# Perceiver block, one core: VectorE's routing, small copies and rounding change places, and eight scatters run ahead of the scan inputs

## What is computed

```python
x = x + xattn(layernorm(x), ctx)   # int8-rounded q and output projection, 16 heads, 1601 keys
x = x + mamba(layernorm(x))        # x_proj, softplus(dt), scan over 128 steps as h = a*h + bx, y + x*D
x = x + moe(layernorm(x))          # 64 experts, top 8, capacity 512 rows each; silu(g)*u, down
def _qdq(x):
    s = jnp.maximum(jnp.max(jnp.abs(x), axis=-1, keepdims=True) / 127.0, 1e-08)
    return jnp.clip(jnp.round(x / s), -127.0, 127.0) * s
...
pos = jnp.arange(P) - starts[e_sorted]
valid = pos < C
xbuf = jnp.zeros((E, C, D)).at[e_sorted, pos].set(x[tok_sorted], mode='drop')
```

## Time and profile before

| what | us |
|---|---|
| median of 3 runs | 2214.68 |
| lowest and highest | 2214.42, 2221.53 |
| the profiled execution, its own time | 2217.85 |
| its span, first to last instruction | 2216.1 |
| start of the first strip's exponential | 37.3 |
| start of the last strip's exponential | 1710.7 |
| pair i = 8, exponential of its first strip to that of the next pair's | 106.3 |

### The profile page before, as it was taken

How to read it: one execution, slowest core, us unless ns; L and a number is a source line. 1 busy time by engine, 2 the same in 40 slices (tenths; PEclk the granted TensorE clock), 3 DMA queues, 4 the chain that set the end, 5 groups by cost and what they waited for, 6 DMA issues and landing times. The chain is left out here.

```text
span 2216.1 us, 52422 instructions
## 1 busy us (share of the span) xinstructions
PE 2017.7 (91%) x19018; PEld 1569.5 (71%) x19018; DVE 1770.3 (80%) x3649; ACT 1603.9 (72%) x3269; POOL 639.2 (29%) x604
## 2 busy tenths in 40 slices
PE   7999999999999999999999999999998459989965
PEld 6777777777777777777777777777775348878854
DVE  5558898989898989898988888888879747767746
ACT  4778787878787878787878787777778237767753
POOL 0002040404131313132221314040303137767760
PEclk9999999999999999999999999999999669999989
DMA  6888783434333343343433334343422147676738
GB/s 196 279 279 278 243 287 113 132 102 113 110 97 112 94 119 95 115 108 107 106 113 103 118 90 132 82 129 79 127 49 86 66 134 223 212 227 210 221 128 341
DMA packets 189535, 330.04 MB, mean 149 GB/s; under 512 B 37771, under 2 KB 154167, under 8 KB 183136
## 3 DMA queue, kind: packets, MB, share of 16 engines
q1 hardware_dynamic: 170848, 291.99, 43.8%
q0 software_dynamic: 18432, 34.69, 4.4%
HBM read 165.53 MB, written 108.27 MB: 124 GB/s over the span
## 5 line engine op out<-in xcount | busy, mean ns | idle before, releaser
L864 ACT ACTIVATE sb_probsT<-W 128x384 f32<-128x384 f32 (+1 forms) x1024 | 475.6, 515 | 84.2 <-PE W L678 79.4
L1055 DVE TENSOR_REDUCE sb_negmax<-S 128x1 f32<-128x1608 f32 x256 | 468.2, 1829 | 77.6 <-PE S L668 75.9
L872 ACT ACTIVATE sb_probs<-S,sb_negmax 128x1608 f32<-128x1608 f32 x256 | 410.1, 1602 | 135.9 <-DVE sb_negmax L1055 135.0
L678 PEld LDWEIGHTS W<-sb_ident,sb_probs 128*128 128x128 f32 (+1 forms) x3328 | 359.3, 139 | 174.2 <-ACT sb_K_f L856 111.3
L678 PE MATMUL W<-sb_ident,sb_probs 128*128 128x128 f32 (+1 forms) x3328 | 472.8, 280 | 9.3 <-DVE sb_z L1142 4.0
L1443 POOL DMA_INDIRECT y_scratch<-sb_ys,sb_places x256 | 254.0, 992 | 107.5 <-issue 74.3
L856 ACT ACTIVATE sb_K_f<-W,sb_k_cols 128x402 f32<-128x402 f32 x256 | 153.9, 601 | 159.1 <-PE W L641 159.0
L550 POOL TENSOR_TENSOR sb_bx<-sb_u,sb_BC 128x512 f32<-128x512 f32 x120 | 178.4, 1502 | 281.0 <-DVE sb_u L1209 210.7
L668 PE MATMUL S<-sb_K,sb_Q 32*128 32x402 f32 (+1 forms) x2048 | 246.1, 552 | 10.9 <-ACT sb_probs L872 9.6
L696 PE MATMUL O<-sb_probsT,sb_V 128*32 128x128 f32 (+1 forms) x6656 | 245.1, 277 | 0.0
L696 PEld LDWEIGHTS O<-sb_probsT,sb_V 128*32 128x32 f32 (+1 forms) x6656 | 174.0, 110 | 47.8 <-issue 45.3
(11 more groups left out here) (209 smaller groups left out, 3655.9 us busy)
## 6 DMA issues: line engine op xcount, KB each, us to landing
sb_ctx<-ctxT SPq DMA_DIRECT2D x128, 402.0 KB, 4.2
sb_K<-sb_K_f SPq DMA_DIRECT2D x1024, 50.2 KB
xe_scratch<-sb_none SPq DMA_DIRECT2D x32, 1088.0 KB, 5.3
sb_xg<-xe_scratch SPq DMA_DIRECT2D x64, 544.0 KB, 4.0
sb_BC<-bc_scratch SPq DMA_DIRECT2D x32, 1024.0 KB, 7.5
sb_Q<-sb_q_own SPq DMA_DIRECT2D x128, 128.0 KB, 3.5
y_scratch<-sb_none SPq DMA_DIRECT2D x16, 1024.0 KB, 5.9
sb_rows<-y_scratch SPq DMA_DIRECT2D x16, 1024.0 KB, 8.1
```

The lines of the kernel that those rows point to most:

```text
L678: ins = pe.transpose(W[0:keys_in(t), at * P:(at + 1) * P], probs[n % 2][:, t * P:t * P + keys_in(t)], ident[:])
L864: act.activation(probsT[k][n % (k + 1)][:, 0:wide], ring[bank_of("T", G, k)][:, 0:wide], ACT.Copy)\
L872: act.activation(probs[n % 2][:].rearrange("p (c k) -> p c k", c=QUADS), scores_of, ACT.Exp, bias=negmax[:, slot:slot + 1], accum_out=den[ ...
L1055: dve.tensor_reduce(negmax[:, slot:slot + 1], scores_of, AX.XY, ALU.max, negate=True).then_inc(max_done, 1)
```

## The change

It gives small jobs other places, moves VectorE's copies of place-2 jobs ahead of the next slot's maximum, moves `z` (m = 3) ahead of the maximum of slot 7, moves the whole routing into slot 6, moves the rounding of the next queries (`round_q`, L964 to L966) from slot 4 to slot 7, puts the copy of `oqT` behind the maximum of slot 5, and has GpSimd issue the eight scatters in one run ahead of all scan inputs. No instruction is added or taken away.

```diff
-FREED_FIRST = (5, 10)
-MIX = {(4, 0): ["O3"], (5, 0): ["oqT"], (5, 1): ["proj"], (6, 0): ["ln2T"], (6, 1): ["xp"], (7, 0): ["dt"],
-       (9, 0): ["XQ"], (9, 2): ["Q"], (10, 0): ["O0"], (14, 0): ["O1"], (1, 0): ["yT"],
-       (2, 0): ["O2", "ln3T"], (2, 1): ["logits"], (3, 2): ["pos"]}
+MIX = {(4, 0): ["O3"], (5, 0): ["oqT"], (5, 1): ["proj"], (6, 0): ["ln2T"], (6, 1): ["xp"], (6, 2): ["dt"],
+       (8, 2): ["XQ"], (9, 2): ["Q"], (10, 2): ["O0"], (14, 2): ["O1"], (1, 0): ["yT"], (1, 2): ["O2"],
+       (2, 0): ["ln3T"], (2, 1): ["logits"], (3, 2): ["pos"]}
...
-            def scatter(p, part):
+            def scatter(p):
...
-                for t in range(part * TOPK // 4, (part + 1) * TOPK // 4):
+                for t in range(TOPK):
...
+                if ended:
+                    scatter(i - 2)
                 if prev and i < PAIRS:
                     for unit in range(UNITS // 2):
                         scan_input(i - 1, unit)
                 if nxt:
                     part_q(i + 1)
-                for part in range(4):
-                    if ended and i != PAIRS:
-                        scatter(i - 2, part)
-                    if prev and i < PAIRS:
-                        scan_input(i - 1, UNITS // 2 + part)
...
+                if prev and i < PAIRS:
+                    for unit in range(UNITS // 2, UNITS):
+                        scan_input(i - 1, unit)
...
-                for job in small_at(G, 0) if slot in FREED_FIRST else []:
+                for job in small_at(G - 1, 2) if G > 0 else []:
                     if job[0] == "O":
                         norm_o(job[1])
-                    if job[0] == "oqT":
-                        copy_out("oqT", p, oqT[:].rearrange("p k t -> p (k t)"))
+                    if job[0] == "XQ":
+                        x_up(job[1])
+                    if job[0] == "Q":
+                        q_out(job[1])
+                if mix and m == 3:
+                    rest_a(p, m, link)
                 if G < ALL_STRIPS:
                     strip_max(G)
...
-                if slot == 8 and 2 <= i < PAIRS:
-                    route_end(i - 2, route_link)
+                if slot == 6 and 2 <= i < PAIRS:
+                    route_link = route_begin(i - 2)
+                if slot == 7 and nxt:
+                    round_q(q_link)
                 if mix and m == 15:
                     rest_a(p, m, link)
                 if mix:
                     rest_b(p, m, link)
...
                 if slot == 6 and 2 <= i < PAIRS:
-                    route_link = route_begin(i - 2)
+                    route_end(i - 2, route_link)
                 if part_at(G, PART_AT):
                     part_low(*part_at(G, PART_AT))
-                if slot == 9 and nxt:
-                    q_out(i + 1)
...
-                if slot == 4 and nxt:
-                    round_q(q_link)
```

More of the change, by code:

```diff
@@ L551, in scan_input @@
                                    ALU.mult).then_inc(pool_up, 1)
-            def scatter(p, part):
-                if p == 0 and part == 0:
+            def scatter(p):
+                if p == 0:
                     pool.wait_ge(xe_clear, 16 * CLEARS)
[L557 to L560, removed]
-                for t in range(part * TOPK // 4, (part + 1) * TOPK // 4):
+                pool.wait_ge(routed, p + 1)
+                pool.tensor_tensor(pause_p[:], neg_half[:], neg_half[:], ALU.add).then_inc(idx_seen, 1)
+                pool.wait_ge(idx_seen, p + 1)
+                for t in range(TOPK):
                     pool.indirect_dma_start(
@@ L583, in _ @@
                     part_q(i + 1)
-                for part in range(4):
-                    if ended and i != PAIRS:
-                        scatter(i - 2, part)
-                    if prev and i < PAIRS:
-                        scan_input(i - 1, UNITS // 2 + part)
-                if i == PAIRS:
-                    for part in range(4):
-                        scatter(i - 2, part)
+                if prev and i < PAIRS:
+                    for unit in range(UNITS // 2, UNITS):
+                        scan_input(i - 1, unit)
             pool.wait_ge(scattered, 16 * TOPK * PAIRS)
@@ L1286, in _ @@
                 v = values_at(G)
-                for job in small_at(G, 0) if slot in FREED_FIRST else []:
+                for job in small_at(G - 1, 2) if G > 0 else []:
+                    if job[0] == "O":
+                        norm_o(job[1])
+                    if job[0] == "XQ":
[4 more added lines that the diff above has]
+                    rest_a(p, m, link)
+                if G < ALL_STRIPS:
+                    strip_max(G)
+                if m == 0:
+                    link = Chain(dve, dve_b, p, B_LINKS, pause[:]) if mix else None
+                for job in small_at(G, 0):
                     if job[0] == "O":
@@ L1291, in _ @@
                         copy_out("oqT", p, oqT[:].rearrange("p k t -> p (k t)"))
[L1292 to L1298, removed]
-                if slot == 9 and nxt:
-                    x_up(i + 1)
-                if mix and m < 15:
+                if mix and m < 15 and m != 3:
                     rest_a(p, m, link)
```

## The result

The changed kernel takes 2180.93 us (median of 4 runs, 2179.32 to 2185.54) against 2214.82 before (4 runs): ratio 0.9839, 95% interval 0.9823 to 0.9855. The profiled execution took 2179.32 us; its first and last exponentials start at 38.1 and 1672.3.

A forecast was written before the change was run, and what follows sets the result against it. TensorE's work plus about 5 us of waits bounds a pair; 3.7 us removed less 2.05 added less 1.0 for the scatter run, over 14 pairs, plus 1.65 for pair 1, gave some 11 us less: 2203.5 us, range 2190 to 2230.

The forecast's parts named there:

- fourth rival: Slot 9: GpSimd is done before the scan arrives, or the scan goes first; 25 us faster, 2190 us, chance 0.10.
- w: V of slot 10 waits for Q's copy: R - 10.5 us per pair beyond R = 10.5, forecast 1.0 us.
- slot 9, K: K in slot 9 no longer stands three places behind XQ, so its wait goes: 1.05 us gained per pair.
- slot 11, K: Scatters leave the later inputs, slot 10's scan takes 1.23 us again, K's wait goes: 1.75 us gained per pair.
- slot 2, ln3T: ln3T now stands three places behind O2 and waits for its copy: 0.5 us lost per pair, ends 0 and 0.7.
- slot 8, K and XQ: K waits 0.6 us for V, XQ 0.4 us for a turn: 1.0 us lost per pair, ends 0.5 and 1.4.
- slot 11, V for O0: V now stands three places behind O0, whose copy is late: 0.45 us lost per pair, ends 0 and 0.8.
- R: Time GpSimd's run of eight scatters takes: forecast 11.5 us; gain turns to loss at 12.15.
- the BC broadcast: Its issue in slot 6 was to hold the scatter run at most 1.3 us; 0.7 us was put down.
- the quiet run: The undisturbed run of eight scatters after the last strip in the profile before, 9.98 us, the base for R.
- The first rival: The scatter run is stretched as in the busy one after the last strip, 14.35 us: 2244 us, chance 0.20.
- The second: Rival: every scatter is held 0.77 us by a VectorE instruction, R = 16.2, 55 us slower, 2270 us, chance 0.08.

The follow-up runs named there:

- e5: The changed kernel with the rounding of the next queries put back at the end of slot 4: 2186.32 us.
- e12: The kernel before with the whole routing moved into slot 6 and nothing else: 2197.5 us.
- e2: The kernel before with the whole routing in slot 6 and the eight scatters in one run ahead of the inputs: 2192.16 us.
- e1: The kernel before with the small jobs and their copies (with z) at the new places; routing, rounding and scatters as before: 2219.37 us.
- e6: The changed kernel with O1 alone back at its old place in slot 14, between the second turn and V: 2191.21 us.
- e9: The changed kernel with the whole routing one slot earlier, in slot 5: 2185.44 us.
- e13: The kernel of e11 with the second half of routing moved ahead of the copy of dlT in slot 6: 2186.99 us.
- e11: The changed kernel with O0 in slot 12, O2 in slot 0, and routing's first half in slot 5, its second in slot 6: 2178.07 us.
- e3: The changed kernel with GpSimd's order of before, scatters by twos between the later inputs: 2199.84 us.
- e4: The changed kernel with the first four scan inputs ahead of the eight scatters and the spread queries behind them: 2230.55 us.

## Why the forecast was right in direction and wrong in size

Its mechanism held: the indices come early, the run of scatters fits into GpSimd's idle time, VectorE's piles in slots 8 and 10 go, and the end of the run comes back through Q's copy at V of slot 10. The result lies beyond the fourth rival's time, and not by its mechanism (w = 0). The steps of the forecast, first by what became of each:

| step | forecast, us | after |
|---|---|---|
| slot 5, proj | -0.45 | gone; e5 prices it at 0.35 |
| slot 7, third turn | -0.45 | gone |
| slot 9, K | -1.05, by XQ's move | gone, by the routing (e12) |
| slot 11, K | -1.75, by the run | gone (e2); the jobs alone rename it (e1) |
| slot 9, Q | +0.1 | waits 0.25, was 0.40 |
| O1's turn in slot 14 | not seen | -0.6 (e6) |
| slot 2, ln3T | +0.5 | waits 0.30 |
| slot 8, K and XQ | +1.0 | wait 0.47 and 0.14 |
| slot 11, V for O0 | +0.45 | waits 0.62 |
| w, V of slot 10 | +1.0 (R = 11.5) | waits 0.59 (R = 11.02) |

Then by stretches of pair 8, from the start of one slot's scores to that of another's, which hold idle and busy time together:

| stretch | forecast, us | before | after | change |
|---|---|---|---|---|
| slots 1 and 2 (O2, ln3T) | +0.5 | 12.93 | 12.94 | 0.0 |
| slot 5 (proj) | -0.45 | 8.01 | 7.65 | -0.36 |
| slots 6 and 7 (third turn) | -0.45 | 13.87 | 13.33 | -0.54 |
| slots 8 to 12 (all other terms) | -0.25 | 34.50 | 33.43 | -1.07 |
| slot 14 (O1) | none | 6.68 | 6.06 | -0.62 |
| the other five slots | none | 30.30 | 30.32 | 0.0 |
| the pair | -0.65 | 106.29 | 103.73 | -2.56 |

Of the 1.9 us that the forecast missed in a pair, 0.8 lie in slots 8 to 12, 0.6 in slot 14 and 0.5 in slots 1 and 2.

**What failed first is the list of what the change takes away,** which put one term at nothing. It was taken from the large waits alone. O1 stood between the second turn and V of slot 14, and V waited there for a turn that ScalarE was still copying. The wait before, and the window of slot 14:

```profile
966.42 0.52 PE L653 MATMUL W<-sb_wkv_hi,sb_ctx_hi 128*128 128x256 f32 x2 [0.30 <-ACT sb_probsT L864]
```
```profile
964.26:970.94 6.68, 6.38 (x65) 4.89 (x65) 6.28 (x13) 5.58 (x13) 0.00 (x0) 1.00 0.25 62
```

That shows as 0.30 us of idle time, and the slot lost twice that (e6 gives the same price). O0 left the same place in slot 10; no run prices that alone.

**What failed second is the costs added,** 3.05 us in the forecast. `ln3T` was to cost 0.5. It waits 0.30, but O2 no longer stands ahead of it in its slot, and slots 1 and 2 together take what they took. In slots 8 to 12 the forecast had 2.55 us of costs; the waits there come to 1.67 (0.61 for K and XQ, 0.59, 0.62, and 0.15 less for Q), idle times without the restart that its terms include. R was nearly right: 11.02 to 11.04 in most pairs instead of 11.5. None of the 0.7 us put down for the BC broadcast came, since the second scatter starts 0.30 us behind the first; VectorE's work cost 1.04 us over the quiet run's 9.98, where the forecast had 0.8. By the forecast's own rule R = 11.02 gives w = 0.52, and V of slot 10 waits 0.59: the path through Q's copy was right, the size of R was not.

The first rival's run stayed where it was, after the last strip (14.28 us there after the change). The second fails too: of the eight scatters one is held by 0.7 us (1.66, beside `part_low`), the others by 0.16 at most. The Trainium skill (SBUF — State Buffer, section "SBUF: two separate sides") warns that a DMA issued from GpSimd cannot write its descriptors while VectorE holds the shared port pair. The trace agrees in that one scatter, and in no other by more than 0.16 us.

**What failed third is the clock.** Three pairs of before held a stretch at half clock after the wait of slot 11. Taking that wait away gave 1.4 to 2 us more in each, some 5 us that a sum of waits doesn't contain. Two pairs at the ends went the other way: pair 1, without scatters, was to gain 1.65 us and lost 0.35, and pair 15 was to gain 0.65 and lost 0.3; why is open.

The attribution was wrong as well, though the sum does not show it: the slot 9 wait was ascribed to XQ's new place, but it was the routing ahead of the maximum. e1 shows the jobs' places worth nothing while the routing stays late; with early routing, e2 to the changed kernel, they and the rounding give 0.4 us. The stretches show why so little: from e2 to the changed kernel slots 8 to 12 grow again by 1.0 us (32.43 to 33.43), and slot 5, slots 6 and 7, and slot 14 give 0.35, 0.43 and 0.59.

What stays open: why a wait of the same length is followed by half clock in some pairs only, and why a run of inputs that had to wait for u (e12, e9) takes 6.4 us and lets `part_low` through at 0.99, while a run right behind the scatters takes 5.0 and holds it. GpSimd and VectorE in e12:

```profile
914.96 6.45 POOL L550 TENSOR_TENSOR sb_bx<-sb_u,sb_BC 128x512 f32<-128x512 f32 x4 [15.04 <-DVE sb_u L1209]
```
```profile
918.05 0.99 DVE L1041 TENSOR_TENSOR sb_ctx_lo<-sb_ctx,sb_ctx_hi 128x804 fp32r<-128x804 f32 x1
```

## What to carry to other kernels

Price the place of a small job by the distance of the starts around it, or by undoing one move on the chip, and not by idle time alone: O1's place showed 0.30 us of idle time, and 0.6 were to be had. When two engines hold each other up, the collision can be moved but hardly removed, so put it behind the operation that the critical engine waits for: the same four inputs cost 0.6 us behind the maximum and, as an estimate, 1.4 ahead of it (the 0.8 that e13 loses to e11, and the 0.59 that went). And read the granted clock after each long wait, pair by pair, before summing waits.

## What the runs showed of the hardware

- GpSimd's elementwise operations, one right behind the other, held a two-input operation of VectorE until the last of them ended: a scan 3.00 instead of 1.23 us, `part_low` 4.45 instead of 0.99, a 128x128 sum 2.97 instead of 0.29 (it began 0.5 us ahead of them, beside the last scatter). The Trainium skill (SBUF — State Buffer, section "SBUF: two separate sides") has the lock held for one instruction, which would be at most 1.25 us here, as an estimate (a quarter of the 4.99 us for four); the measurement goes beyond that, and the exception is the open point above.
- After a wait of 1.65 to 1.93 us in slot 11 TensorE's clock fell to half in 3 of 13 pairs of before, 3 of e1, 2 of e12 and 10 of e3, at about 1.4 us each (2.0 in one pair of before); after 3.3 us in all 13 (e4); after 0.93 us in none (e2).
